# First slots of an eight-layer attention and expert kernel in a new order on five engines

## What is computed

```python
x = x + attn(_layernorm(x), ...)     # eight layers, each:
    q = phi((h @ wq + bq)); k = phi((h @ wk + bk)); v = h @ wv + bv      # phi = elu + 1, 16 heads of 8
    kv = sum over tokens of k v;  z = 1 / (q . sum(k) + 1e-6)
    h = ln(h + (q kv z) @ wo + bo) * g1 + be1
    h = ln(h + gelu(h @ w1 + c1) @ w2 + c2) * g2 + be2
x = x + ffn(_layernorm(x), ...)      # norm, router, top 2 of 8 experts, silu, weighted sum, residual
```

## Time and profile before

| | us |
|---|---|
| median of three runs | 1069.81 (1069.41 to 1070.71) |
| the profiled execution's own time | 1069.99 |
| its span, first to last instruction | 1068.3 |
| TensorE matmul busy | 994.1 |
| slot 0 of layer 0 on TensorE | 15.91 to 38.19 |
| slot 1 | 38.19 to 62.42 |

### The profile page before, as it was taken

How to read it: one execution, slowest core, us unless ns; L and a number is a source line. 1 busy time by engine, 2 the same in 40 slices (tenths; PEclk the granted TensorE clock), 3 DMA queues, 4 the chain that set the end, 5 groups by cost and what they waited for, 6 DMA issues and landing times.

```text
span 1068.3 us, 25009 instructions
## 1 busy us (share of the span) xinstructions
PE 994.1 (93%) x7558; PEld 928.7 (87%) x7558; DVE 820.3 (77%) x2710; ACT 832.2 (78%) x1621; POOL 769.6 (72%) x1157
## 2 busy tenths in 40 slices
PE   5799999999999999999999999999998849989983
PEld 4799989999999999999999999899997749889983
DVE  6777887888888888887888788788888988952514
ACT  5778887888888888888888888888886655665572
POOL 5767886787877778777777677777765677677752
PEclk9999999999999999999999999999999969999997
DMA  4101263126314431453145216401100345667785
GB/s 140 50 2 36 44 138 62 36 67 119 59 36 97 90 60 42 98 92 58 42 102 106 50 41 138 85 2 21 22 2 1 98 146 148 177 202 215 205 258 158
DMA packets 198499, 94.65 MB, mean 89 GB/s; under 512 B 120124, under 2 KB 179523, under 8 KB 198368
## 3 DMA queue, kind: packets, MB, share of 16 engines
q1 hardware_dynamic: 193824, 84.59, 33.9%
q0 software_dynamic: 4544, 8.47, 2.3%
HBM read 44.82 MB, written 29.44 MB: 70 GB/s over the span
## 4 chain that ended last, share of the span: by engine, by line
PE 73%; POOL 6%; issue 5%; DVE 4%; SPq 4%; DMA 4%; ACT 3%; POOLq 0%; DVEq 0%
PE psum L1907 19%; PE psum L1784 8%; PE psum L1785 8%; PE psum L1786 8%; PE psum L1831 6%; PE psum L1865 5%; PE psum L1837 5%; PE psum L1819 4%; POOL xs L915 4%; PE psum L2064 4%; PE psum L2048 4%; SPq L498 2%; DMA this_w<-w 1%; DMA xblk<-xs 1%; DVE stat L1218 1%
## 5 line engine op out<-in xcount | busy, mean ns | idle before, releaser
L1012 ACT ACTIVATE s<-s,shift,rstd 128x128 f32<-128x128 f32 x496 | 203.9, 486 | 40.6 <-POOL shift L747 40.1
L1907 PE MATMUL psum<-this_w,hid 128*128 128x128 f32 x1792 | 216.3, 277 | 2.4 <-DMA this_w<-w 2.2
L1907 PEld LDWEIGHTS psum<-this_w,hid 128*128 128x128 f32 x1792 | 208.5, 193 | 3.2 <-DMA this_w<-w 3.2
L991 ACT ACTIVATE hid<-psum,col 128x512 f32<-128x512 f32 x256 | 155.4, 684 | 2.2 <-PE psum L1786 1.7
L745 POOL TENSOR_TENSOR rstd<-var,neg_half 128x4 f32<-128x4 f32 x132 | 146.3, 1108 | 11.0
L788 POOL TENSOR_TENSOR res_a<-s,row 128x512 f32<-128x512 f32 x60 | 77.3, 1288 | 73.8 <-ACT s L1012 68.6
L1218 DVE BATCH_NORM_STATS2 stat<-s 128x6 f32<-128x128 f32 x512 | 110.0, 276 | 0.0
L742 POOL TENSOR_SCALAR shift<-mv 128x4 f32<-128x4 f32 x132 | 26.0, 197 | 99.9 <-DVE mv L1222 98.6
L1784 PE MATMUL psum<-x_hi,this_w 128*128 128x512 f32 x224 | 95.4, 426 | 1.2 <-DVE x_lo L1290 1.2
L773 POOL TENSOR_TENSOR res_f<-res_f,row 128x512 f32<-128x512 f32 x64 | 92.3, 1443 | 5.0
L2064 PE MATMUL psum<-heads,hid 128*128 x624 | 84.7, 279 | 5.5 <-ACT hid L1144 5.2
(11 more groups left out here) (264 smaller groups left out, 2747.7 us busy)
## 6 DMA issues: line engine op xcount, KB each, us to landing
xs<-pad SPq DMA_DIRECT2D x18, 975.0 KB, 8.8
feature<-xrow SPq DMA_DIRECT2D x416, 32.0 KB, 2.0
res_a<-w SPq DMA_DIRECT2D x40, 256.0 KB
xblk<-xs SPq DMA_DIRECT2D x78, 65.0 KB
raw_w<-w SPq DMA_DIRECT2D x18, 256.0 KB, 3.1
row<-rows SPq DMA_DIRECT2D x8, 512.0 KB, 5.2
this_w<-next_w SPq DMA_DIRECT2D x7, 512.0 KB, 3.2
third_w<-w SPq DMA_DIRECT2D x10, 256.0 KB, 7.3
```

The lines of the kernel that those rows point to most:

```text
L991: a.activation(hid[h][:, c, :], ps(3 + h + c), ACT.Gelu, bias=col[:, bass.ds(lw * FF + (C_C1 + c), 1)]).then_inc(hid_done, 1)
L1012: ins = a.activation(dst[:, t, :], src[:, t, :], ACT.Identity, bias=shift[i][:, t:t + 1], scale=rstd[i][:, t:t + 1])
L1907: ins = t_.matmul(ps(down_bank(l, s, h))[:, t * P:(t + 1) * P], hid[h][:, c, t * P:(t + 1) * P], down[:, c, :], start=c == 0, stop=c == FF ...
```

## The change

- SP issues half 1 of x right behind half 0, ahead of the table and the weights. The router's matrix and one row share a semaphore, `late_in`.
- TensorE first does twelve products of a constant tile with itself (`keep_clock`), then `bias_products(0)`, now into bank 6, then the flips of halves 0 and 1, each followed by four more constant products. The results of the constant products are not used.
- ScalarE loads its table at the start, with an activation on a constant.
- The normalised rows go to `res_a` instead of `hid`. `start_resid(u)` adds the bias row in place, behind the flip, and has a semaphore of its own, `first_resid`. Gelu waits no more for the residuals.
- POOL does `start(1)` ahead of the scaling of the first weights.
- The first steps of pairs 2 and 3 are spread out: statistics, inverse and norm of halves 4 and 5 at the end of slot 0, of halves 6 and 7 in slot 1; flips, high and low parts of halves 4 and 5 in slot 1, of 6 and 7 in slot 2; the first residuals of pair s in slot s.
- Flips of halves 4 to 7 wait for a chunk of gelu, whose bank they use.

```diff
+        def bias_bank(l):
+
+            return 1 if l else 6
...
-            return hid[u % 2][:, u // 2, :].rearrange("p (t n) -> p t n", t=T)
+            return res_a[:, u]
...
-        START_BANK = (4, 5, 6, 7, 6, 7, 4, 5)
+        START_BANK = (4, 5, 6, 7, 4, 5, 4, 5)
...
             sp.dma_start(x_all[:, 0], x[0]).then_inc(x_in[0], 16)
+            sp.dma_start(x_all[:, 1], x[1]).then_inc(x_in[1], 16)
             sp.dma_start(col[:, :], cols).then_inc(col_in, 16)
             load_raw(0)
-            sp.dma_start(x_all[:, 1], x[1]).then_inc(x_in[1], 16)
             load_rows(0, 0)
...
             def start_resid(u):
                 pool.wait_ge(x2_done, u + 1)
-                g.tensor_tensor(res_a[:, u], first_norm(u), rows_of(R_BIN, 0), ALU.add).then_inc(resa_done, 1)
+                pool.wait_ge(t2_mm, u + 1)
+                g.tensor_tensor(res_a[:, u], first_norm(u), rows_of(R_BIN, 0), ALU.add).then_inc(first_resid, 1)
             start(0)
+            start(1)
             pool.wait_ge(col_in, 16)
             scale_qkv(0)
-            start(1)
             start(2)
             start(3)
             scale_w1(0)
-            for u in range(4, HALVES):
-                start(u)
             hi_w1(0)
             lo_w1(0)
             sum_rows(0, 0)
             wait(pool, rows_summed, 8)
-            for u in range(HALVES // 2):
-                start_resid(u)
+            start_resid(0)
+            start_resid(1)
+            start(4)
+            start(5)
...
                 if p1:
                     inv_std1(l, s - 1, 0)
                     inv_std1(l, s - 1, 1)
-                    if first and s == 1:
-                        for u in range(HALVES // 2, HALVES):
-                            start_resid(u)
                     resid_f(l, s - 1, 0)
                     resid_f(l, s - 1, 1)
+                    if first:
+                        start_resid(2 * s)
+                        start_resid(2 * s + 1)
+                    if first and s == 1:
+                        start(6)
+                        start(7)
...
             def gelu(l, s, h):
                 lw = layer_at(l, s)
-                if l == 0:
-                    wait(act, resa_done, HALVES)
...
+            act.wait_ge(const_step, 7)
+            a.activation(warm[:, 0:1], ones[:, 0:1], ACT.Exp).then_inc(exp_table, 1)
+            start(0)
             act.wait_ge(raw_in, 32)
             a.activation(this_qkv[:, 0, :], raw_qkv[:, :], ACT.Copy).then_inc(qkv_split, 4)
-            start(0)
             start(1)
...
                     start_split(2)
                     start_split(3)
-                    for u in range(4, HALVES):
-                        start(u)
-                    start_split(4)
-                    start_split(5)
...
                 flips = p2 and flipped(l, s - 2)
+                if first and 1 <= s < 3:
+                    start_split(2 * s + 2)
+                    start_split(2 * s + 3)
...
-                load_table(ACT.Exp, 1, exp_table, l * SLOTS + s)
+                load_table(ACT.Exp, 1, exp_table, l * SLOTS + s + 1)
                 if flips:
                     split_xt(l, s - 2, 1)
-                if first and s == 0:
-                    start_split(6)
-                    start_split(7)
+                if first and s < 2:
+                    start(2 * s + 4)
+                    start(2 * s + 5)
...
             start(2)
+            start_lo(0)
             start(3)
-            start_lo(0)
             start_lo(1)
             biases(0, 0)
-            start(4)
-            start(5)
-            start(6)
...
                 if first and s == 0:
-                    start_lo(4)
-                    start_lo(5)
+                    start_lo(3)
+                if first and s < 2:
+                    start(2 * s + 4)
+                    start(2 * s + 5)
...
                 if flips:
                     lo_xt(l, s - 2, 0)
+                if first and 1 <= s < 3:
+                    start_lo(2 * s + 2)
+                    start_lo(2 * s + 3)
...
-                    wait(pe, xt_lo_done, (2 if s == 0 else HALVES) if first and s < 3 else banks_upto(l, s - 3))
-                elif h == 0 and ((s == 3 and not last) or (first and s == 0)):
-                    wait(pe, bias_done, l * 8 + (16 if s == 3 else 8))
+                    wait(pe, xt_lo_done, 2 * s + 2 if first else banks_upto(l, s - 3))
+                elif h == 0 and s == 3 and not last:
+                    wait(pe, bias_done, l * 8 + 16)
...
+            def start(u):
+
+                pe.wait_ge(x2_done, u + 1)
+                if u == 2:
+                    pe.wait_ge(bias_done, 8)
+                elif u >= 4:
+                    pe.wait_ge(hid_done, upto(0, u // 2 - 2, 1, per=FF) - 3 + u % 2)
+                flip(START_BANK[u], first_norm(u)).then_inc(t2_mm, 1)
+
+            def keep_clock(n):
+
+                for _ in range(n):
+                    t_.matmul(ps(3)[:, 0:P], ones[:, :], ones[:, :], start=True, stop=True)
+
+            pe.wait_ge(const_step, 7)
+            keep_clock(12)
             pe.wait_ge(const_done, 1)
...
+            bias_products(0)
             start(0)
+            keep_clock(4)
             start(1)
-            bias_products(0)
+            keep_clock(4)
...
-                if first and s == 0:
-                    start(4)
-                    start(5)
                 flip_att(l, s, 0)
+                if first and 1 <= s < 3:
+                    start(2 * s + 2)
+                    start(2 * s + 3)
...
                 if first and s == 0:
-                    pe.wait_ge(xt_lo_done, 6)
+                    pe.wait_ge(xt_lo_done, 4)
                 out_proj(l, s, 0)
                 out_proj(l, s, 1)
-                if first and s == 0:
-                    start(6)
-                    start(7)
```

More of the change, by code:

```diff
@@ L130, in resid_upto @@
     l, p = ORDER[l * SLOTS + s]
-    return HALVES + (2 * ORDER.index((l - 1, p)) + h + 1 if l else 2 * p + h + 1 - HALVES)
+    return 2 * ORDER.index((l - 1, p)) + h + 1 if l else 2 * p + h + 1
 def flips_upto(i, h):
@@ L363, in build @@
         x_in = [sem(f"x_in{u}") for u in range(HALVES)]
-        col_in, row_in, router_in = sem("col_in"), sem("row_in"), sem("router_in")
+        col_in, row_in, late_in = sem("col_in"), sem("row_in"), sem("late_in")
         raw_in, last_in = sem("raw_in"), sem("last_in")
@@ L392, in build @@
         resf_mul, resf_done, resa_mul, resa_done = (sem(n) for n in ("resf_mul", "resf_done", "resa_mul", "resa_done"))
-        offset_done, mv0_done, std0_done, outer_done, bef_in = (
-            sem(n) for n in ("offset_done", "mv0_done", "std0_done", "outer_done", "bef_in"))
+        offset_done, mv0_done, std0_done, outer_done, first_resid = (
+            sem(n) for n in ("offset_done", "mv0_done", "std0_done", "outer_done", "first_resid"))
         p_step, mvg_done, std_done, fin_ready = (sem(n) for n in ("p_step", "mvg_done", "std_done", "fin_ready"))
@@ L483, in _ @@
                 sp.dma_start(x_all[:, u], x[u]).then_inc(x_in[u], 16)
-            sp.dma_start(r_raw[:, :], router).then_inc(router_in, 16)
-            sp.dma_start(bef[:, :], rows[LAYERS, R_B1 * P:(R_B1 + 1) * P].partition_broadcast(P)).then_inc(bef_in, 16)
+            sp.dma_start(r_raw[:, :], router).then_inc(late_in, 16)
+            sp.dma_start(bef[:, :], rows[LAYERS, R_B1 * P:(R_B1 + 1) * P].partition_broadcast(P)).then_inc(late_in, 16)
             set_wo(0)
@@ L797, in prep_router @@
             def prep_router():
-                pool.wait_ge(router_in, 16)
+                pool.wait_ge(late_in, 32)
                 g.tensor_scalar(r_sc[:, :], r_raw[:, :], col[:, C_GAMMA:C_GAMMA + 1], 0.0, ALU.mult, ALU.add).then_inc(r_prep, 1)
@@ L826, in _ @@
             wait(pool, rows_summed, 8)
-            for u in range(HALVES // 2):
-                start_resid(u)
+            start_resid(0)
+            start_resid(1)
+            start(4)
+            start(5)
             def offset_input(u):
                 if u == 0:
-                    pool.wait_ge(bef_in, 16)
+                    pool.wait_ge(late_in, 32)
                 pool.wait_ge(x2_done, u + 1)
@@ L1275, in add_res1 @@
                 wait(dve, wo_mm, upto(l, s, h))
-                wait(dve, resa_done, resid_upto(l, s, h))
+                wait(dve, resa_done if layer_at(l, s) else first_resid, resid_upto(l, s, h))
                 wait(dve, t1_mm, upto(l, s - 1, h))
@@ L1334, in biases @@
                 wait(dve, row_in, l * 16 + 16)
-                b = ps(1)
+                b = ps(bias_bank(l))
                 kvb = row[:, ring, R_BK:R_BK + 2, :]
@@ L1388, in stack_moments @@
                 if u < T:
-                    wait(dve, resa_done, HALVES + 2 * ORDER.index((LAST, u // 2)) + u % 2 + 1)
+                    wait(dve, resa_done, 2 * ORDER.index((LAST, u // 2)) + u % 2 + 1)
                 half_moments(0, u, res_a, mv0_done)
```

9 lines of the change are left out of this document (1 added, 8 removed).

## The result

The changed kernel took a median of 1078.35 us (1074.38 to 1081.64, 7 runs); the kernel before beside it took 1069.41 (1067.96 to 1070.86, 7 runs). The ratio is 1.008 [1.006, 1.0101]: slower by 8.9 us, where +3.65 was forecast and +7.2 was the end of the range.

A forecast was written before the change was run, and what follows sets the result against it. TensorE, busy 994.1 of 1068.3 us, was taken to bound the kernel from slot 2 of layer 0 on. The terms -1.9 + 1.75 + 2.0 + 1.8 gave +3.65 us, 1073.5 us; range 1067.8 to 1077.0.

The forecast's parts named there:

- The start of TensorE: Before slot 0's attention: bias products from 9.2 us at the lower clock, projection at 17.1 against 15.91.
- Rival 1: First flips and projection: constant products hold clock; slot 1's attention gains 4.3 us; chance 0.08 with POOL's waits, 0.13 hidden.
- Attention of slot 1 at 49.5: 1.9 us gained: Layer 0, slot 1: attention starts at 49.5 us instead of 51.44; bounds 0 and about 4.3 gained.
- yardstick: Start of attention in slot 1, 51.44 us before: gain there, less what TensorE gets later, is the result.
- Moved past the bound: Slots 1 and 2: four flips that lay in idle time now cost TensorE +1.75 us.
- Slot 2's new wait: Slot 2: two POOL residuals delay the inverse, norm2 and gelu, so TensorE waits for a gelu chunk; +2.0 us.
- Slot 3: Slot 3: two more POOL residuals delay the next slot's inverse, norm1 and TensorE's flip; +1.8 us, bounds 0 and 2.5.
- Rival 2: Slots 2 and 3: POOL's residuals are hidden, only -1.9 + 1.75 us is left, 1069.7 us; chance 0.19.
- Rival 3: Slots 2 and 3: the new waits cost the clock too, 1.65 us a fall, 1075.1 or 1076.8 us; chance 0.15.
- Rival 4: Start: constant products lift nothing and the start is later, gain 0 at slot 1, 1075.4 us; chance 0.07.

The follow-up runs named there:

- e9: The changed kernel without POOL's wait for x2_done in start_resid; 1076.70 us, ratio 1.0062.
- e2: The changed kernel without any of the 20 constant products; 1075.96 us, ratio 1.0093.
- e3: The kernel before with only the early part of the change, pairs 2 and 3 in slot 0 as before; 1068.38 us, ratio 1.0007.
- e6: The kernel before with eight long-met waits added in POOL's list; 1070.08 us, ratio 1.0005.
- e7: The changed kernel with residuals at the head of POOL's slots, no constant products, halves 4 and 5 wholly in slot 1; 1070.43 us, ratio 1.0009.
- e12: e10 with one POOL wait for late_in fewer, first indirect DMA at 1347; 1068.61 us, ratio 0.9983.
- e13: The kernel before with one long-met POOL wait added, first indirect DMA at 1348; 1072.45 us, ratio 1.0028.
- e1: The changed kernel with the first residuals at the head of POOL's slots 1 to 3; 1074.97 us, ratio 1.0065.
- e4: The changed kernel with the early order put back, only the late part kept; 1076.25 us, ratio 1.0078.
- e10: e7 without POOL's wait for x2_done in start_resid; 1070.14 us, ratio 1.0004.
- e14: The changed kernel without constant products, with residuals at the head of POOL's slots and first indirect DMA at 1347; 1070.93 us, ratio 1.0013.
- e5: The changed kernel with more unused products in TensorE's waits of slots 0 and 1; 1077.21 us, ratio 1.0069.
- e11: e5 with residuals at the head of POOL's slots, four filling products in slot 1, no x2_done wait in start_resid; 1075.96 us, ratio 1.0061.

## Why the prediction was wrong

The direction was right, and so were the two largest of the steps that cost. The size was wrong in one term of the sum, and one cost was missing.

**The start of TensorE**: bias products from 9.80 (9.2 forecast), at the lower clock, projection at 16.91 (17.1), keys at 19.37 (19.4). `boff` took 0.76 us, not 0.39, which is most of the 0.6. The constant products did not hold the clock: after the wait of 3.35 us the bias products took 1.19 us and the first flip 1.09, as at the start of the kernel before (1.12). Rival 1 is out. That activity had raised the clock and idle time lowered it again is seen in e9, where the bias products at 9.87, behind a wait of 2.87 us, still took 0.67 us (1.19 in e2, which has no constant products), and the granted clock was 1.00 to 10.4 and 0.50 from 10.6. The rule of the Trainium skill (TensorE: Matmul & The Clock Gate, "The HAM clock gate") that idle throttles again what activity has released agrees with it. The twelve constant products ended too long before anything that could use the clock.

**The failed step is "Attention of slot 1 at 49.5: 1.9 us gained".** It started at 52.55, 1.1 lost: 3.0 us off, by three pieces, the largest of them a fall of TensorE's clock that the forecast priced at nothing.
- In slot 0 the clock fell to half in the wait of 1.76 us ahead of the second key_value. The last attention result started at 32.27; without the fall it was 30.65 (e2). 1.6 us, which the forecast priced at nothing: a wait of 1.55 us had left the clock up, and no chance was given to its falling in one of 1.76. The length of the wait doesn't decide it, nor do the constants: behind waits of 1.72 to 1.76 us in this place the clock stayed up in e2, e3, e6, e7, e9, e12 and e13 and fell in the changed kernel, e1, e4, e10 and e14. Of these e3, e9, the changed kernel and e1 have the constant products. e9 differs from the changed kernel by POOL's waits alone and had attention at 51.02; e12 differs from e10 by one of POOL's waits. So in this slot it falls in some executions and not in others.
- The stretch from the keys to the end of the last attention result was taken as 11.0 us, from 19.4 to 30.4. In e2 it took 11.6, from 19.72 to 31.34: 0.9 us later. The low part, the two statistics (ended at 33.1 and 34.3, not 32.2 and 33.4) and the two inverses behind it took what was forecast, so that ScalarE's first query of slot 1 came at 38.43 in e2 against 37.5, the same 0.9 us.
- From the flip of slot 1 to attention it was 8.4 us (44.16 to 52.55; in e2 8.3, 42.53 to 50.81) against 7.26 before: 1.0 to 1.1 lost to the clock behind the wait of 4.29, where 0.6 was taken.

The yardstick had a fault of its own. The 51.44 of the kernel before holds a fall of the clock, in the 3.25 us of its output products, and the forecast used that row as a price of the lower level without asking what the landmark would be otherwise. Versions of that kernel which kept the clock there had 50.17 and 49.63 (e6, e13). Against them the 49.5 of the forecast was a gain of 0.1 to 0.7 us, not of 1.9, and the changed kernel's 52.55 is 2.4 to 2.9 late, not 1.1.

**Moved past the bound, +1.75**: 1.76 in e14. Right.

**Slot 2's new wait, +2.0**: 2.11, in the place named and by the chain named. Right; the step from slot 2 to slot 3 is 3.3 longer with one pair's flips in it, so 0.3 more than the sum. e1 shows it causally.

**Slot 3, +1.8**: 1.4 of wait, 1.5 in the landmark. Right in place, and gone in e1. Rival 2 is out.

These come to +6.8 at layer 1's first attention, against +3.65: the failed step makes up nearly all of the difference.

**What was missing** lies behind the main part: the gap, 1.70 us in the trace (e9 closed it and no other; its ratio is 1.0062 against 1.008, within each other's intervals, but e13 puts a gap of 3.0 at 0.28% [0.08, 0.48], 0.9 to 5 us). The forecast counted POOL's work, and the waits it adds not at all. The rest of the +11.4, about 2 us behind the first expert flip, can't be put down to the change: from that flip to the end the kernels took 197.6 to 201.8 us, with no order by what they change.

Rival 3 (the two new waits cost the clock too) didn't happen in the changed kernel's trace; in e4 and in e5 slot 2's wait did. Rival 4 had the size of slot 1's loss nearer (no gain), though the clock was up at the changed kernel's projection (0.48 us for its first product, 0.77 in e2); the flips and waits came on top of it as forecast.

## What to carry to other kernels

When a step is moved off a stretch that waits, follow it on the engine that isn't the bound: POOL's two additions had to stand ahead of a part that was waiting, not ahead of an inverse that two engines and the tail of a slot wait for, and that place alone was worth 4 us in the traces. Price a new or longer wait on TensorE with the clock in it, as a chance and not as a yes or no, and take several traces before a clock fall is put down to an edit. The trace of the kernel before is one draw as well: look for falls in it before a landmark of it becomes the yardstick. When a change adds as little as a wait to a list, look at every idle stretch marked "issue" behind it: a cost of 2 us can sit at the other end of the program, and one instruction more or less moves it.

## What was not expected of the hardware

- POOL's idle time ahead of its first indirect DMA depends on the place of that DMA in POOL's list: 0.71 us at 1347 (five kernels: before, e3, e9, e12, e14), 2.97 to 3.08 at 1348 (e10, e11, e13), 2.12 at 1351, 1.88 to 2.67 at 1354 (seven kernels).
- TensorE's clock fell behind waits of one length in one kernel and not in its near twin: in slot 0 behind 1.72 to 1.76 us in five kernels and not in seven, in slot 2 behind 2.11 us in e4 and e5 and not in the changed kernel, e2 and e9, and behind 1.62 in the kernel before and not in e6, e13 and e3. A fall cost about 1 to 2 us in these places, in e5 3.2.
- Early in a trace, ahead of its first change, the granted clock in a window's row doesn't tell TensorE's speed. Bias products in e2 and in the changed kernel, windows from 10 to 12 us:

```profile
10.00:12.00 2.00, 2.00 (x9) 1.00 1.05 399
```

```profile
10.00:12.00 2.00, 2.00 (x9) 0.50 1.04 390
```

```profile
9.85 1.19 PE L1928 MATMUL psum<-raw_qkv,boff 128*128 128x256 f32 x2 [9.85 <-POOL boff L710]
```

The row says 1.00 in e2 and 0.50 in the other, and the same pair of products took 1.19 us in both. In e9, where the clock fell only at 10.5, it took 0.67:

```profile
9.87 0.67 PE L1927 MATMUL psum<-raw_qkv,boff 128*128 128x256 f32 x2 [2.87 <-POOL boff L710]
```

Durations of a known product are what to go by.
- `boff`, 128x128 on POOL, took 0.39 us in the kernel before and 0.76 in the changed one, with the same shape and operands; by how much the neighbours on the other engines slow it was not tried.
